# Row maxima of two score steps subtracted by four products on row tiles of 32

## The chip, the cores and the metric

The kernel runs on one core of one Trainium2 chip. The metric is the device time of one execution in microseconds. Before the change it was 839.73 us (median of 3 runs, 839.26 to 842.45).

## The reference, cut to what matters

Two batches of 1024 tokens with 128 features pass a modulated normalisation, an attention with 16 heads of 64 features, a second modulated normalisation and a mixture of 8 experts. What the change touches is the softmax of the attention:

```python
scores = jnp.einsum('bhqd,bhkd->bhqk', q, k) * scale
attn = jax.nn.softmax(scores, axis=-1)
out = jnp.einsum('bhqk,bhkd->bhqd', attn, v)
```

For each batch and head there are 1024 queries and 1024 keys. The softmax needs each query's maximum score subtracted before the exponential.

## The kernel before

**Pairs, steps and groups.** Two heads of one batch form a pair, and there are 16 pairs (`NPAIR`). The 64 features of head 0 lie on partitions 0 to 63 and those of head 1 on partitions 64 to 127. A pair's work on scores is 16 steps (`NSTEP`): 2 halves of 512 queries times 8 tiles of 128 keys. A step makes, for both heads, the scores of 128 keys (on partitions) by 512 queries in two PSUM banks. Even steps write banks 0 and 1 of `ps_s`, odd steps banks 2 and 3. Two steps form a group; a pair has 8 groups (`NGRP`), so there are 128 groups in all.

**The products of a step** (`score`, L472 to L478). q and k are each split into an upper part in TensorE's rounded float type and a rest. A step adds three products for each head, k_hi·q_hi, k_lo·q_hi and k_hi·q_lo, and a fourth, `one_row`·`neg_row` (L478), which adds minus the maximum of each query to all 128 keys. `one_row` is zero except for a row of ones at partition 0 and one at partition 64; `neg_row` holds minus the maxima of head 0 at partition 0 and of head 1 at partition 64, and zero elsewhere. Each of these products contracts over 64 partitions, so the two heads' products stand on two different halves of the array's rows and are issued one behind the other. ScalarE takes the exponential of the finished banks (`expo`, L784).

**The maxima.** A rough product of the next pair (`maxima`, L451) is reduced by VectorE (`reduce_max`, L1219), two in each group, 16 for a pair. After 8 of them, `neg_max` (L1224) gives minus the maxima of half the queries of both heads, with queries on partitions. `max_rows` on the SP queue (L1531) lays them out as rows: 8 small DMAs for a half, one for each head and 128 queries. TensorE waits for them at the first step of the half (`row_placed`).

**The order on TensorE** is written out by hand. In a group of a pair before the last it is: `maxima(p+1, 2g)`, `score(p, 2g)`, `score(p, 2g+1)`, `maxima(p+1, 2g+1)`, `up(p+2, g)` (L439, a piece of q or k of the pair after next), then the values times the probabilities of the group before (`pv`, L488). In group 0 the denominators of the pair before follow (L497), in groups 4 and 6 its outputs (L539). `maxima` waits until VectorE has reduced the one before it. The last pair has no `maxima` and no `up`, but sums of probabilities on TensorE (L506).

**The order on VectorE** in a group g of pair p: `reduce_max(p+1, 2g)`, `lower` (L1212), `reduce_max(p+1, 2g+1)`, in groups 3 and 7 `neg_max`, then `turn` (L1201 to L1206). In group 1, behind `turn`, stands `recip(p-1)` (L1261), which waits for the denominators of the pair before to have landed with queries on partitions (`den_cols_in`). In groups 3 and 5 stand `divide` (L1267).

**The order on the SP queue** for a pair p > 0: `max_rows(p, 1)`, `den_cols(p-1)` (4 DMAs, L1540, which wait for ScalarE's copy of the denominators), `inv_rows`, `inv_spread`, then `max_rows(p+1, 0)` and the weights of pair p+4. For the last pair, 8 loads of expert weights (L1558) stand between `max_rows` and `den_cols`.

**Tiles of the array.** The shapes in the profile tell which part of the array's rows a product takes: 64\*128 a product over 64 partitions, 128\*128 one over all, 128\*64 and 128\*32 products whose results go to 64 or 32 partitions, 1\*128 a product over a single partition (L690, in the experts' part).

Of the kernel before, what the change touches and what calls it, by code (L numbers as in the profile page):

```python
# [10 lines left out]
F32 = mybir.dt.float32  # L11
# [3 lines left out]
P = 128  # L15
# [3 lines left out]
TB = S // P  # L19
HP = H // 2  # L20
NPAIR = B * HP
HALF = 512
# [22 lines left out]
def ge(eng, sem, value):  # L45

    if value > 0:
        eng.wait_ge(sem, value)


def build(nc, t, out):
    ctx = ExitStack()
    with ctx:
        def sb(name, shape, dt=F32):
            return ctx.enter_context(nc.sbuf_tensor(name, shape, dt))

        def pb(name, shape=(P, HALF), dt=F32):
            return ctx.enter_context(nc.psum_tensor(name, list(shape), dt))

        def sem(name):  # L60
            return ctx.enter_context(nc.semaphore(name))
# [42 lines left out]
        q_hi = sb("q_hi", [P, 3, S], F32R)  # L104
        q_lo = sb("q_lo", [P, 3, S], F32R)
        k_hi = sb("k_hi", [P, 3, S], F32R)
        k_lo = sb("k_lo", [P, 3, S], F32R)
        hi_of, lo_of = (q_hi, k_hi), (q_lo, k_lo)
        one_row = sb("one_row", [P, P], F32R)
        neg_row = sb("neg_row", [P, 2, S], F32R)  # L110
# [66 lines left out]
        ps_s = pb("ps_s", (P, 4, HALF))  # L177
# [86 lines left out]
        s = {n: sem("s_" + n) for n in signals}  # L264
# [5 lines left out]
        row_placed = [sem(f"row_placed{n}") for n in range(2)]  # L270
# [14 lines left out]
        def n_step(p, st):  # L285
            return NSTEP * p + st + 1
# [10 lines left out]
        def n_part(p, half):  # L297
            return 2 * p + half + 1

        def n_den(p, half=0):  # L300

            return p + 1 + (half if p == LAST else 0)
# [4 lines left out]
        def quarter(j):  # L307
            return slice(32 * j, 32 * j + 32)
# [12 lines left out]
        def lowers(q):  # L321

            return (s["pool_lower"], 4) if q == 1 else (s["lower"], all_units(q))
# [25 lines left out]
        def rows(h):  # L349
            return slice(64 * h, 64 * h + 64)  # L350


        T_FEAT, T_LOG, T_CN, T_SCAT, T_DVE = (0, 2), (1, 3), 5, 3, 6

# [20 lines left out]
        def _(pe):  # L375
# [3 lines left out]
            for b in range(B):  # L379
                for n in range(2):  # L380
                    nc.tensor.matmul(ps_s[:, 2 * b + n, 0:3 * D], c_rep[:, b, :], wmod_sb[:, n * 3 * D:(n + 1) * 3 * D],
                                     start=True, stop=True).then_inc(s["mod_product"], 1)
# [59 lines left out]
            def maxima(q, n):  # L442
# [9 lines left out]
                                           k_hi[rows(h), q % 3, kh * HALF:(kh + 1) * HALF], start=True, stop=True)  # L452
                ins.then_inc(s["max_product"], 1)

            def score(p, st):

                half, kt = divmod(st, TB)
                if st == 0:
                    pe.wait_ge(*lowers(p))
                ge(pe, s["probs"], n_step(p, st) - 2)  # L460
                if kt == 0:
                    pe.wait_ge(row_placed[half], 128 * (p + 1))
                if p > 0 and st == (5 if p == LAST else 3):
                    pe.wait_ge(s["den_read"], n_den(p - 1))
                if 0 < p < LAST and st in (11, 15):
                    pe.wait_ge(s["out_added"], n_part(p - 1, st == 15))
                if p == LAST and st == 13:
                    pe.wait_ge(s["out_added"], n_part(p - 1, 0))
                kc, qc = slice(kt * P, (kt + 1) * P), slice(half * HALF, (half + 1) * HALF)
                bank = [ps_s[:, 2 * (st % 2) + h, :] for h in range(2)]  # L470
                for h in range(2):
                    nc.tensor.matmul(bank[h], k_hi[rows(h), p % 3, kc], q_hi[rows(h), p % 3, qc], start=True, stop=False)  # L472
                for h in range(2):
                    nc.tensor.matmul(bank[h], k_lo[rows(h), p % 3, kc], q_hi[rows(h), p % 3, qc], start=False, stop=False)  # L474
                for h in range(2):
                    nc.tensor.matmul(bank[h], k_hi[rows(h), p % 3, kc], q_lo[rows(h), p % 3, qc], start=False, stop=False)  # L476
                for h in range(2):
                    ins = nc.tensor.matmul(bank[h], one_row[rows(h), :], neg_row[rows(h), p % 2, qc], start=False, stop=True)  # L478
                ins.then_inc(s["scores"], 1)

            def pv(p, st):

# [121 lines left out]
            for p in range(NPAIR):  # L604
                for g in range(NGRP):
                    if p < LAST:
                        maxima(p + 1, 2 * g)
                    score(p, 2 * g)
                    score(p, 2 * g + 1)
                    if p < LAST:  # L610
                        maxima(p + 1, 2 * g + 1)
# [503 lines left out]
        def _(dve):  # L1115
            seq = [0]
            V = nc.vector

            def then(ins):

                seq[0] += 1
                ins.then_inc(s["vector_step"], 1)
                dve.wait_ge(s["vector_step"], seq[0])
# [1 line left out]
            V.memset(ones[:], 1.0)  # L1125
            V.memset(one_row[:].bitcast(F32), 0.0)
            then(V.memset(neg_row[:].bitcast(F32), 0.0))
            V.memset(one_row[0:1, :].bitcast(F32), 1.0)
            V.memset(one_row[64:65, :].bitcast(F32), 1.0).then_inc(s["constants"], 1)
            then(V.memset(head_row[:], 0.0))  # L1130
            for n in range(4):
                V.memset(head_row[32 * n:32 * n + 1, n // 2:n // 2 + 1], 1.0)
# [35 lines left out]
            for b in range(B):  # L1168
                ins = V.tensor_copy(c_rep[:, b, :], c_e[:, 0, b:b + 1].to_broadcast([P, P]))
# [50 lines left out]

            def neg_max(q, half):
                dve.wait_ge(s["max_reduced"], NMAX * q + TB * (half + 1))
                ge(dve, row_placed[half], 128 * q)
                V.tensor_reduce(nm[:, half, :, :], mx[:, :, :, 4 * half:4 * half + 4].rearrange("p h k t -> p h t k"),  # L1224
                                AX.X, ALU.max, negate=True).then_inc(s["max_row"], 1)

# [20 lines left out]
            for n in range(8):  # L1247
# [4 lines left out]
                if n == 3:  # L1252
                    inverse(T1, 4)
            neg_max(0, 0)
            for n in range(8, NMAX):
                reduce_max(0, n)
            neg_max(0, 1)

            def recip(p):
# [81 lines left out]
            row = lambda a: a.unsqueeze(1).to_broadcast([P, TB, E])  # L1341
# [77 lines left out]
            for p in range(NPAIR):  # L1419
                for g in range(NGRP):  # L1420
                    if g == 5 and 1 <= p < LAST:
                        out_add(p - 1, 0, ps_s[:, 3, :])
                    if g == 7 and 1 <= p < LAST:
                        out_add(p - 1, 1, ps_s[:, 3, :])
                    if p < LAST:
                        reduce_max(p + 1, 2 * g)
                    q, u = (p + 2, g - 1) if g else (p + 1, NGRP - 1)
                    if 2 <= q <= LAST:
                        lower(q, u)
                    if p < LAST:  # L1430
                        reduce_max(p + 1, 2 * g + 1)
                        if g % 4 == 3:
                            neg_max(p + 1, g // 4)
                    if p + 2 <= LAST:
                        turn(p + 2, g)
                    if 0 < p < LAST:
                        if g == 1:
                            recip(p - 1)
                        if g == 3:
                            divide(p - 1, 0)  # L1440
                        if g == 5:
                            divide(p - 1, 1)
                    if p == HP + 1:
                        if g in (2, 4):
                            block_stats(T0[2 * g - 4:2 * g])
                        if g == 6:
                            block_norm(T0)
            p = LAST
# [69 lines left out]
        def _(sp):  # L1518
# [4 lines left out]
            def max_rows(q, half):  # L1523

                sp.wait_ge(s["max_row"], 2 * q + half + 1)
                if q >= 2:
                    sp.wait_ge(s["scores"], n_step(q - 2, TB * half + TB - 1))
                for h in range(2):
                    for n in range(4):
                        row = neg_row[64 * h:64 * h + 1, q % 2, half * HALF + n * P:half * HALF + (n + 1) * P]  # L1530
                        sp.dma_start(row.bitcast(F32), nm[:, half, h, n:n + 1].bitcast(F32)).then_inc(row_placed[half], 16)  # L1531

            def den_cols(p, halves):
# [53 lines left out]
            weights(2)  # L1587
            sp.wait_ge(s["constants"], 1)
            max_rows(0, 0)
            max_rows(0, 1)  # L1590
            weights(3)

# [105 lines left out]
```

## Time and profile before

| | |
|---|---|
| median of 3 runs | 839.73 us |
| the profiled execution's own time | 843.6 us |
| its span from first to last instruction | 841.7 us |
| mean granted TensorE clock | 0.984 of full speed |
| PE busy | 806.4 us, 96% |
| PEld busy | 481.3 us, 57% |
| DVE busy | 618.2 us, 73% |
| ACT busy | 394.2 us, 47% |
| POOL busy | 652.0 us, 77% |
| L478 (`one_row`·`neg_row`) | 512 products, 101.4 us |
| L1531 (`max_rows`) | 256 DMAs |

PE is TensorE's matmul side and PEld its weight loads, DVE is VectorE, ACT ScalarE, POOL GpSimd, SPq the DMA queue of SyncE. The ends of matmuls are modelled, so that two of them overlap on paper; their starts are what tells their pace. L478 is line 478 of the kernel printed above.

### The profile page before, as it was taken

The page shows a single profiled execution, that of the slowest core. Times are in us where ns is not written, and L with a number is a line of the kernel's source. Part 1 is how long each engine was busy: PE and PEld are TensorE (multiplying, and loading weights), DVE is VectorE, ACT ScalarE, POOL GpSimd, SP SyncE. Part 2 cuts the span into 40 slices and gives each one's busy share as a digit, 9 for nine tenths or more (in the row PEclk, how much of TensorE's full clock was granted, in tenths as well). Part 3 has the DMA queues.
Part 4 walks back from the last instruction along what each step waited for, and adds up shares of the span by engine and source line. Part 5 has one row for each costly group of instructions (what it writes and reads, how often), then busy time and mean ns, then how long its engine had stood idle before and what let it go on. Part 6 is the DMA issues. An engine that isn't in the chain of part 4 may idle for free.

```text
span 841.7 us, 15143 instructions
## 1 busy us (share of the span) xinstructions
PE 806.4 (96%) x5218; PEld 481.3 (57%) x5218; DVE 618.2 (73%) x1204; ACT 394.2 (47%) x636; POOL 652.0 (77%) x341
## 2 busy tenths in 40 slices
PE   4878999999999999999999999999999999999986
PEld 2535556555555555555555555555565555448886
DVE  8887777787778787878777877778777756346644
ACT  3655444444444444444444445544444444435543
POOL 3479998999999797979797989888888787041654
PEclk8979999999999999999999999999999999999989
DMA  9600010101001010101010101010101010452763
GB/s 246 144 1 14 14 27 14 28 14 25 15 13 28 2 39 2 38 3 39 1 39 2 39 1 40 1 27 15 28 1 27 1 27 1 127 181 80 243 217 97
DMA packets 83257, 40.00 MB, mean 48 GB/s; under 512 B 57433, under 2 KB 71136, under 8 KB 83120
## 3 DMA queue, kind: packets, MB, share of 16 engines
q1 hardware_dynamic: 81456, 35.86, 17.9%
q0 software_dynamic: 1728, 3.19, 1.0%
q8 instruction: 43, 0.70, 0.3%
q14 instruction: 30, 0.25, 0.1%
HBM read 31.46 MB, written 8.21 MB: 47 GB/s over the span
## 4 chain that ended last, share of the span: by engine, by line
PE 93%; DVE 3%; DMA 1%; issue 1%; POOL 1%; ACT 0%; POOLq 0%; SPq 0%; DVEq 0%
PE ps_o L488 28%; PE ps_m L451 9%; PE ps_x L439 9%; PE ps_s L472 7%; PE ps_s L474 7%; PE ps_s L478 7%; PE ps_s L476 7%; PE ps_s L539 4%; PE ps_s L677 3%; PE ps_s L497 2%; DVE mx L1219 1%; PE ps_m L506 1%; PE ps_s L687 1%; PE ps_x L687 1%; PE ps_o L687 1%
## 5 line engine op out<-in xcount | busy, mean ns | idle before, releaser
L1040 POOL TENSOR_TENSOR big<-big,probs 128x1024 f32<-128x1024 f32 x180 | 440.3, 2446 | 70.0 <-ACT probs L784 49.9
L1219 DVE TENSOR_REDUCE mx<-ps_m 128x2 f32<-128x1024 f32 x240 | 294.0, 1225 | 108.5 <-PE ps_m L451 108.2
L784 ACT ACTIVATE probs<-ps_s 128x1024 f32<-128x1024 f32 x256 | 248.9, 1024 | 169.1 <-PE ps_s L478 169.0
L488 PE MATMUL ps_o<-probs,c_all 128*64 128x512 f32 x1024 | 247.9, 605 | 0.0
L488 PEld LDWEIGHTS ps_o<-probs,c_all 128*64 128x64 f32 x1024 | 62.1, 136 | 97.2 <-ACT probs L784 41.4
L451 PE MATMUL ps_m<-k_hi,q_hi 64*128 64x512 f32 x480 | 108.4, 444 | 2.2 <-DVE mx L1219 2.2
L472 PE MATMUL ps_s<-q_hi,k_hi 64*128 64x512 f32 x512 | 101.8, 393 | 0.0
L478 PE MATMUL ps_s<-neg_row,one_row 64*128 64x512 f32 x512 | 101.4, 388 | 0.0
L474 PE MATMUL ps_s<-q_hi,k_lo 64*128 64x512 f32 x512 | 101.2, 390 | 0.0
L476 PE MATMUL ps_s<-q_lo,k_hi 64*128 64x512 f32 x512 | 101.2, 389 | 0.0
L451 PEld LDWEIGHTS ps_m<-k_hi,q_hi 64*128 64x128 f32 x480 | 46.6, 183 | 87.3 <-issue 77.0
L1040 POOL TENSOR_TENSOR big<-probs 128x1024 f32<-128x1024 f32 x30 | 71.6, 2386 | 9.9 <-ACT probs L784 9.9
L775 ACT CAST q_hi<-ps_x 128x256 fp32r<-128x256 f32 x56 | 20.9, 372 | 90.6 <-DVE ps_x L1206 90.6
L478 PEld LDWEIGHTS ps_s<-neg_row,one_row 64*128 64x128 f32 x512 | 48.8, 184 | 10.5
L476 PEld LDWEIGHTS ps_s<-q_lo,k_hi 64*128 64x128 f32 x512 | 48.4, 184 | 10.7
L474 PEld LDWEIGHTS ps_s<-q_hi,k_lo 64*128 64x128 f32 x512 | 48.4, 184 | 10.3
L472 PEld LDWEIGHTS ps_s<-q_hi,k_hi 64*128 64x128 f32 x512 | 48.6, 185 | 9.6 <-issue 3.3
L1102 POOL DMA_INDIRECT out_dram<-c_all,token x30 | 29.8, 993 | 29.1 <-DVE c_all L1483 20.9
L1206 DVE TENSOR_TENSOR ps_x<-ps_x,big 128x256 f32<-128x256 f32 x112 | 48.5, 433 | 3.8
L1276 DVE TENSOR_TENSOR h<-h,ps_s 128x512 f32<-128x512 f32 x29 | 20.0, 688 | 40.2 <-PE ps_s L539 39.6
L1201 DVE TENSOR_TENSOR ps_x<-ps_x,big 128x256 f32<-128x256 f32 x112 | 47.3, 423 | 0.0
L1204 DVE TENSOR_TENSOR big<-ps_x,big 128x256 f32<-128x256 f32 (+1 forms) x113 | 47.2, 417 | 0.0
(310 smaller groups left out, 997.3 us busy)
## 6 DMA issues: line engine op xcount, KB each, us to landing
big<-in_experts SPq DMA_DIRECT2D x30, 322.0 KB, 3.6
big<-rd_dram SPq DMA_DIRECT2D x60, 128.0 KB, 2.9
big<-in_wqk SPq DMA_DIRECT2D x16, 256.0 KB, 2.7
neg_row<-nm SPq DMA_DIRECT2D x256, 0.5 KB, 2.0
xs_row<-xs_dram SPq DMA_DIRECT2D x6, 390.0 KB, 4.2
big<-in_expert_w SPq DMA_DIRECT2D x8, 256.0 KB, 4.0
xs_dram<-zero SPq DMA_DIRECT2D x2, 990.0 KB, 10.4
xs_dram<-zero SPq DMA_DIRECT2D x2, 960.0 KB, 11.7
```

The lines of the kernel that those rows point to most:

```text
L439: ins = nc.tensor.matmul(bank, m[:, q % 2, w, twin, :], src, start=(n == 0), stop=(n == 1))
L451: ins = nc.tensor.matmul(bank[:, h, :], q_hi[rows(h), q % 3, qt * P:(qt + 1) * P], k_hi[rows(h), q % 3, kh * HALF:(kh + 1) * HALF], start= ...
L472: nc.tensor.matmul(bank[h], k_hi[rows(h), p % 3, kc], q_hi[rows(h), p % 3, qc], start=True, stop=False)
L474: nc.tensor.matmul(bank[h], k_lo[rows(h), p % 3, kc], q_hi[rows(h), p % 3, qc], start=False, stop=False)
L476: nc.tensor.matmul(bank[h], k_hi[rows(h), p % 3, kc], q_lo[rows(h), p % 3, qc], start=False, stop=False)
L478: ins = nc.tensor.matmul(bank[h], one_row[rows(h), :], neg_row[rows(h), p % 2, qc], start=False, stop=True)
L488: ins = nc.tensor.matmul(ps_o[64 * h:64 * h + 64, :], c_all[:, (p // HP) * TB + kt, :], probs[:, st % 4, h, :], start=(kt == 0), stop=(kt ...
L784: nc.scalar.activation(probs[:, st % 4, :, :], ps_s[:, 2 * (st % 2):2 * (st % 2) + 2, :], ACT.Exp, scale=SCALE).then_inc(s["probs"], 1)
L1040: V.tensor_tensor(acc[:, buf(p, half), :, :], first, probs[:, st % 4, :, :], ALU.add).then_inc(s["added"], 1)
L1201: V.tensor_tensor(straight, straight, cos_sb[:, c], ALU.mult).then_inc(s["turned"], 1)
L1206: V.tensor_tensor(straight, straight, part, ALU.add).then_inc(s["rotated"], 1)
L1219: V.reduce_max(mx[:, :, kh, qt], max_banks(q, n), AX.X).then_inc(s["max_reduced"], 1)
```

## The change

The constants: `one_row` has a row of ones at each of the partitions 0, 32, 64 and 96. `max_rows` places the negated maxima of head 0 at partitions 0 and 32, and those of head 1 at 64 and 96, for every pair but the first; for the first only at 0 and 64 as before. A half of a pair thus has 16 small DMAs in place of 8, and the counts that wait on them follow (`n_rows`).

On TensorE the two products at L478 go from each step. In their place `less_max` stands at the start of the odd step, behind that step's waits. It issues four products, each over 32 partitions: two that end the even step's banks, and two that begin the odd step's banks. In pairs after the first these four stand on the four different row tiles of 32; in the first pair the even and the odd step's stand on the same two. The wait for `row_placed` moves into `less_max`. The even step's signal is given by the second of the four, and the odd step's by its last k_hi·q_lo.

```diff
+        def n_rows(q):
+            return 128 * (2 * q + 1)
...
+            def less_max(p, st, steps):
+                half = st // TB
+                qc = slice(half * HALF, (half + 1) * HALF)
+                if st % TB == 0:
+                    pe.wait_ge(row_placed[half], n_rows(p))
+                for odd in steps:
+                    for h in range(2):
+                        r = quarter(2 * h + odd if p else 2 * h)
+                        ins = nc.tensor.matmul(ps_s[:, 2 * odd + h, :], one_row[r, :], neg_row[r, p % 2, qc],
+                                               start=(odd == 1), stop=(odd == 0))
+                    if odd == 0:
+                        ins.then_inc(s["scores"], 1)
...
-                if kt == 0:
-                    pe.wait_ge(row_placed[half], 128 * (p + 1))
...
+                odd = st % 2
+                if odd:
+                    less_max(p, st - 1, (0, 1))
                 for h in range(2):
-                    nc.tensor.matmul(bank[h], k_hi[rows(h), p % 3, kc], q_hi[rows(h), p % 3, qc], start=True, stop=False)
+                    nc.tensor.matmul(bank[h], k_hi[rows(h), p % 3, kc], q_hi[rows(h), p % 3, qc], start=not odd, stop=False)
...
-                    nc.tensor.matmul(bank[h], k_hi[rows(h), p % 3, kc], q_lo[rows(h), p % 3, qc], start=False, stop=False)
-                for h in range(2):
-                    ins = nc.tensor.matmul(bank[h], one_row[rows(h), :], neg_row[rows(h), p % 2, qc], start=False, stop=True)
-                ins.then_inc(s["scores"], 1)
+                    ins = nc.tensor.matmul(bank[h], k_hi[rows(h), p % 3, kc], q_lo[rows(h), p % 3, qc], start=False, stop=bool(odd))
+                if odd:
+                    ins.then_inc(s["scores"], 1)
...
-            V.memset(one_row[0:1, :].bitcast(F32), 1.0)
-            V.memset(one_row[64:65, :].bitcast(F32), 1.0).then_inc(s["constants"], 1)
+            for j in range(4):
+                ins = V.memset(one_row[32 * j:32 * j + 1, :].bitcast(F32), 1.0)
+            ins.then_inc(s["constants"], 1)
...
-                ge(dve, row_placed[half], 128 * q)
+                ge(dve, row_placed[half], n_rows(q - 1) if q else 0)
...
-                for h in range(2):
+                for j in (range(4) if q else (0, 2)):
+                    h = j // 2
                     for n in range(4):
-                        row = neg_row[64 * h:64 * h + 1, q % 2, half * HALF + n * P:half * HALF + (n + 1) * P]
+                        row = neg_row[32 * j:32 * j + 1, q % 2, half * HALF + n * P:half * HALF + (n + 1) * P]
```

## Rows read from the trace of the kernel before

**Rows 1.** The page: TensorE's granted clock in 40 slices, in tenths.
```profile
PEclk8979999999999999999999999999999999999989
```

**Rows 2.** The page: the chain that ended last, by engine and by line.
```profile
PE 93%; DVE 3%; DMA 1%; issue 1%; POOL 1%; ACT 0%; POOLq 0%; SPq 0%; DVEq 0%
PE ps_o L488 28%; PE ps_m L451 9%; PE ps_x L439 9%; PE ps_s L472 7%; PE ps_s L474 7%; PE ps_s L478 7%; PE ps_s L476 7%; PE ps_s L539 4%; PE ps_s L677 3%; PE ps_s L497 2%; DVE mx L1219 1%; PE ps_m L506 1%; PE ps_s L687 1%; PE ps_x L687 1%; PE ps_o L687 1%
```

**Rows 3.** Timeline of PE, groups 1 and 2 of a pair: start us, us, instruction, count.
```profile
330.78 0.40 PE L478 MATMUL ps_s<-neg_row,one_row 64*128 64x512 f32 x2
331.01 0.40 PE L451 MATMUL ps_m<-k_hi,q_hi 64*128 64x512 f32 x2
331.34 0.39 PE L439 MATMUL ps_x<-ck,wh 128*128 128x256 f32 x1
331.56 0.28 PE L439 MATMUL ps_x<-ck,wl 128*128 128x256 f32 x1
331.68 0.29 PE L439 MATMUL ps_x<-ck,wh 128*128 128x256 f32 x1
...
332.01 1.94 PE L488 MATMUL ps_o<-probs,c_all 128*64 128x512 f32 x8
333.88 0.50 PE L451 MATMUL ps_m<-k_hi,q_hi 64*128 64x512 f32 x2
334.21 0.39 PE L472 MATMUL ps_s<-q_hi,k_hi 64*128 64x512 f32 x2
...
336.04 0.43 PE L451 MATMUL ps_m<-k_hi,q_hi 64*128 64x512 f32 x2
```

**Rows 4.** Timeline of PE, four products on column tiles of 32.
```profile
110.17 1.06 PE L497 MATMUL ps_s<-big,ones 128*32 128x512 f32 x8
```

**Rows 5.** Timeline of PE, a product over one partition, then products over 128.
```profile
765.17 0.48 PE L690 MATMUL ps_s<-big,ones_sq 1*128 1x128 f32 x2
765.59 1.06 PE L592 MATMUL ps_m<-gw_sb,h2T 128*128 128x8 f32 x8
766.50 1.14 PE L677 MATMUL ps_s<-moe,big 128*128 128x128 f32 x8
```

**Rows 6.** Timeline of the SP queue in the pair of rows 3, and in the last pair.
```profile
321.83 4.99 SPq L1531 DMA_DIRECT2D neg_row<-nm  x8
329.58 2.46 SPq L1540 DMA_DIRECT2D denc<-den  x4
...
712.44 5.16 SPq L1531 DMA_DIRECT2D neg_row<-nm  x8
717.71 4.79 SPq L1558 DMA_DIRECT2D big<-in_expert_w  x8
```

**Rows 7.** Timeline of DVE in the pair of rows 3.
```profile
333.72 0.24 DVE L1261 RECIPROCAL rc<-denc 128x16 f32<-128x16 f32 x1
334.42 1.23 DVE L1219 TENSOR_REDUCE mx<-ps_m 128x2 f32<-128x1024 f32 x1 [0.46 <-PE ps_m L451]
```

**Rows 8.** Timelines of SP, DVE and PE in the last pair but one.
```profile
670.23 4.98 SPq L1531 DMA_DIRECT2D neg_row<-nm  x8
677.30 2.46 SPq L1540 DMA_DIRECT2D denc<-den  x4
681.25 0.25 DVE L1261 RECIPROCAL rc<-denc 128x16 f32<-128x16 f32 x1 [0.85 <-DMA denc<-den]
683.71 0.39 PE L451 MATMUL ps_m<-k_hi,q_hi 64*128 64x512 f32 x2
```

**Rows 9.** Timelines of DVE and PE where PE waits for a reduction.
```profile
68.39 1.23 DVE L1219 TENSOR_REDUCE mx<-ps_m 128x2 f32<-128x1024 f32 x1 [0.83 <-PE ps_m L451]
69.77 0.50 PE L451 MATMUL ps_m<-k_hi,q_hi 64*128 64x512 f32 x2 [0.75 <-DVE mx L1219]
```

**Rows 10.** Timelines of DVE and PE in the last pair.
```profile
737.58 1.29 DVE L1267 TENSOR_TENSOR ou<-ou,big 128x512 f32<-128x512 f32 x2
742.74 1.16 PE L539 MATMUL ps_s<-hT,ou 128*128 128x128 f32 x8
```

## Prediction, made before the changed kernel had run

> **What bounds the kernel now.** I read the chain of waits on the page first. 93% of the span runs through PE, and the lines on it are the ones that the change edits and their neighbours: L472 to L478 have 7% each [rows 2]. The clock row says that this PE runs at the higher of its two levels (2.4 GHz) in nearly all slices [rows 1]. Then I read the timeline of PE through one group, by starts, since ends are modelled. No gap in it is left that another engine causes; the pace is that of PE's own products. So whatever the change takes from or adds to PE's row of starts in a group counts in full, 128 times. Last I read the SP queue and VectorE between two pairs, because the change doubles DMAs there [rows 6 to 8].
>
> **The slot.** Two products of 64 partitions and 512 columns, one for each head, start together, and the next two start 0.23 us later (330.78 to 331.01) [rows 3]. A step has four such slots, so a group has eight, and the two of L478 are worth 0.46 us. The four products of 32 partitions go to four different row tiles and four banks. The nearest row is the one where four products go to four column tiles: its 8 records (4 products in 2 passes) take 1.06 us, where 8 records of L488 on two tiles (four passes) take 1.94 [rows 3, 4]. Four tiles run beside each other as well as two. I take one slot of 0.23 us for the four. The bounds: 0.23, and 0.46 if only two at a time run. Removed, then: 0.46 - 0.23 = 0.23 us in each group after the first pair (15 x 8 = 120 groups), nothing in the first pair's 8 groups, where the four stand on two tiles and need two slots.
>
> **The change of tile size, twice in a group.** No row of before shows a step from 64 rows to 32 and back, but all changes of the tile's shape that the rows show cost alike. From L451 (64\*128) to L439 (128\*128): 331.01 to 331.34 is 0.33, which is 0.10 over the slot, and the first L439 takes 0.22 to the second, which takes 0.12 to the third: 0.10 more. Together 0.20 us. Behind L488 (128\*64) the first L451 (64\*128) takes 0.33 in place of 0.23 (333.88 to 334.21), the same second part [rows 3]. A product over one partition between products over 128 is the row nearest to tiles of 32. From its start, with its weights in the open and the emptying behind it, to the next line it takes 0.42 us (765.17 to 765.59), for two passes, where the passes behind it take 0.91 / 8 = 0.11 each: 0.20 over once more [rows 5]. I read it as two parts: the array empties (0.09 to 0.10), and the first weights of the new shape are loaded in the open, not under the product before (0.10 to 0.11). Two changes in a group cost 2 x 0.20 = 0.40 us. Bounds for one change: 0 (tiles of 64 and of 32 rows might count as one kind), and 0.25 (as above with four loads in the open in place of one or two). I take 0.20, where all the shape changes in the rows lie.
>
> In sum, a group of the later 15 pairs gets 0.40 - 0.23 = 0.17 us longer, one of the first pair 0.40. That is 120 x 0.17 = 20.4 (21 with 0.175) and 8 x 0.40 = 3.2, **24 us in all**.
>
> The Trainium skill (TensorEngine Tiling (Array Packing), Key Properties) says the same in a rule: a switch of tiling mode, not of the tile alone, drains the TensorE, and its list has rows of 64 and of 32 as two modes. The trace agrees for the changes it has, with 0.20 us each [rows 3, 5]. Against it stands another page of the Trainium skill (TensorE: Matmul & The Clock Gate, What overlaps and what doesn't), which has four tiles of 32 rows start about 4 ns apart and weights load under products on other row groups; by it alone a group would be 0.23 us shorter. No run here has shown that for a change of shape.
>
> **The even step's signal** comes from the second of the four, at about the place of its old fourth slot, 0.2 us later by the first change of shape. The odd step's comes 0.17 later. ScalarE and GpSimd follow; the products that need these probabilities (L488) stand one group later, some 5 us. Cost 0. The waits of the odd step (bank read, `den_read`, `out_added`) now stand before the even step is ended, but what they wait for is released by earlier work. Cost 0, at most some 0.1 us in three groups of a pair. The wait for `row_placed` comes 0.7 us later in the group than before: gain 0, as nobody waited there. The two more memsets are about 0.1 us on VectorE at the start, under the loads of the inputs.
>
> **The doubled DMAs.** On the SP queue 8 of them take 4.99 us and 4 of the next kind 2.46, so one more is 0.63 to 0.64 [rows 6]. Bounds: 0.63, and 0 if the issue were not what holds the queue; its constant pace says it is. 16 then take 4.99 + 8 x 0.64 = 10.1 us. Behind them in the queue stand the four `denc<-den` (L1540), which had started at 329.58, when ScalarE's copy was there. Now the queue is free at 321.83 + 10.1 + 0.1 (the step from 717.60 to 717.71 [rows 6]) = 332.07. From the first of these four to the reciprocal it takes 3.95 us where VectorE did nothing but wait (677.30 to 681.25 [rows 8]). So the reciprocal of this pair starts at 336.02 in place of 333.72 [rows 7], 2.3 us later, and VectorE waits at it. What is queued behind it on VectorE is `reduce_max`, due at 334.42. It starts at 336.2, takes 1.23 and ends at 337.43; from such an end to the L451 that waits for it it takes 0.15 (68.39 + 1.23 = 69.62, then 69.77) [rows 9], so PE goes on at 337.58. PE had reached this L451 at 336.04 [rows 3], and with three groups' products 0.175 longer reaches it at 336.57. **PE waits 1.0 us**, in pairs 1 to 13. In pair 14 the same sum gives: queue free at 670.23 + 10.24 = 680.47, reciprocal at 684.42, PE free at 685.98, due at 683.71 + 0.53 = 684.24, so 1.7 us [rows 8]. Together 13 x 1.0 + 1.7 = **15 us**. Bounds: 0 (if the later queue is hidden) to 18, if the queue's way to the first of L1540 is 0.2 us longer in each pair.
>
> Later in the pair nothing is late: all is moved by the same wait, and the queue's next task, `max_rows(p+1, 0)`, has until the pair's end. `row_placed` of half 1 lands 12 us after the first issue and is wanted in group 4, some 20 us after it. In the last pair the expert weights and L1540 start 5.1 us later. VectorE has no maxima left; its divisions at 737.58 come at latest at 742.7 and end at 744.0, and L539 wants them at 742.74 + 5 x 0.175 = 743.6 [rows 10]: at most 0.4 us, which I put at 0.
>
> **The sum.** 24 + 15 = 39 us. Against the profiled execution's own time, 843.6 (span 841.7 and 1.9 around it), that is 882.6. That execution was 3.9 us above the median of the three runs, and the sum goes on the median: 839.7 + 39 = **879 us**.
>
> **Rivals.**
> - Switching costs, but the longer queue is hidden, because VectorE or the landing has slack that I don't see: 839.7 + 24 = 864 us. For it: of these pairs only the one of rows 8 lists a wait at L1261. Against it: the reciprocal starts only 4.14 us behind the first L1540 there, of which 3.95 is the bare way, so the slack was 0.19 us [rows 6 to 8].
> - Tiles of 64 and of 32 rows are one kind, and the change of shape is free, but the queue is late. The products save 120 x 0.23 = 27.6 us. PE is then due at the L451 at 336.04 - 0.69 = 335.35 and waits 2.2 us in 13 pairs and 3.0 in pair 14, 32 us together. Result 844, not clearly slower. For it: no row shows 64 to 32. Against it: the three kinds of change that rows show.
> - The shape change is free and the queue is hidden: 839.7 - 27.6 = 812 us, clearly faster. This needs both; it decides in every group, from a switch of under 0.11 us on, as 2 x 0.115 is the slot that is saved. The same price of 0.20 in all rows speaks against it.
>
> **Chances.** The forecast 0.60; queue hidden (864) 0.14; shape free, queue late (844) 0.13; both free (812) 0.08; something that makes it longer than 890, such as four tiles in two slots (120 x 0.23 = 28 more), 0.05. The forecast's own range is 866 to 890: switches of 0.15 (12 us less) to 0.25, where the queue's wait shrinks as the groups get longer. The range that holds 8 in 10 reaches down to the rival at 844, so 841 to 890. A measurement of this kernel can tell 0.5% (4 us) from no change. Faster by more than that: 0.09. Within: 0.07, which is half of the rival at 844. Slower: 0.84.
>
> **What would show it.** In PE's timeline of a group: the four products start within some 20 ns, 0.33 us behind the last L476, and the next two starts are 0.33 us apart each; a group without extras (334.21 back to the one before at 329 or so) lasts 5.2 us, not 5.03. 16 issues of `neg_row<-nm` take 10.1 us, and the waits list VectorE's reciprocal waiting for `denc<-den` in all pairs, then L451 waiting about 1 us for L1219 in group 2. If the four start 0.23 us behind L476 and the k_hi·q_hi 0.23 us behind them, the switch is free and the forecast wrong; if the L451 of group 2 has no wait, its second part is.

## The result, and the profile after

The changed kernel takes 894.1 us (median of 4 runs, 889.24 to 898.75), the kernel before beside it 840.51. The ratio is 1.0622, with a 95% interval of 1.0583 to 1.066: **slower by 6%**, 53.6 us, where the forecast was 879 and 39 us. The direction and both mechanisms came out as forecast. The sum was too small, and the time lies above the range, which ended at 890.

The chain of waits on the page of the changed kernel, and TensorE's granted clock in 40 slices, which answer to [rows 1, 2]:

```profile
PEclk8979999999999999999999999999999999999999
...
PE 64%; SPq 19%; DVE 8%; DMA 5%; issue 3%; POOL 0%; ACT 0%; POOLq 0%; DVEq 0%
```

PE had 93% of the chain before; now 19% of it is the SP queue, which had nothing. The chain goes back from PE over VectorE to the queue wherever PE waited last. The slices are too coarse to show what the clock did; a window further down does.

PE's timeline of groups 1 and 2 of a pair, as in [rows 3] (start us, us, instruction, count):

```profile
350.28 0.40 PE L491 MATMUL ps_s<-q_hi,k_hi 64*128 64x512 f32 x2
...
355.16 0.50 PE L455 MATMUL ps_m<-k_hi,q_hi 64*128 64x512 f32 x2
355.50 0.40 PE L491 MATMUL ps_s<-q_hi,k_hi 64*128 64x512 f32 x2
...
355.98 0.40 PE L495 MATMUL ps_s<-q_lo,k_hi 64*128 64x512 f32 x2
356.30 0.51 PE L468 MATMUL ps_s<-neg_row,one_row 32*128 32x512 f32 x4
356.74 0.50 PE L491 MATMUL ps_s<-q_hi,k_hi 64*128 64x512 f32 x2
357.08 0.40 PE L493 MATMUL ps_s<-q_hi,k_lo 64*128 64x512 f32 x2
357.31 0.40 PE L495 MATMUL ps_s<-q_lo,k_hi 64*128 64x512 f32 x2
358.40 0.50 PE L455 MATMUL ps_m<-k_hi,q_hi 64*128 64x512 f32 x2 [0.70 <-DVE mx L1238]
```

The four products of L468 are one row and one slot. Into them it takes 0.32 us (355.98 to 356.30), out of them 0.44 (356.30 to 356.74), and the next slot takes 0.34, where each was 0.23. That is 0.09 + 0.21 + 0.11 = 0.41 us for two changes of the tile's shape. The weight loads (PEld) show the part in the open: those of L468 start at the same time as its first product, 356.30, and not under the product before.

```profile
356.30 0.19 PEld L468 LDWEIGHTS ps_s<-neg_row,one_row 32*128 32x128 f32 x4 [0.37 <-issue]
```

The group lasts 5.22 us (350.28 to 355.50), where it was 5.05. Then the second half of the forecast: L455 would have followed L495 after 0.23 us, at 357.54, and starts at 358.40.

The same place on the SP queue and on VectorE, as in [rows 6, 7]:

```profile
342.74 10.13 SPq L1551 DMA_DIRECT2D neg_row<-nm  x16
352.97 2.48 SPq L1560 DMA_DIRECT2D denc<-den  x4
```
```profile
356.93 0.25 DVE L1280 RECIPROCAL rc<-denc 128x16 f32<-128x16 f32 x1 [1.83 <-DMA denc<-den]
357.10 1.16 DVE L1238 TENSOR_REDUCE mx<-ps_m 128x2 f32<-128x1024 f32 x1
```

The 16 DMAs take 10.13 us (forecast 10.1), the reciprocal starts 14.19 us after the first of them (forecast 14.19), and L455 15.66 (forecast 15.75). The list of waits of the whole kernel (us in total, times, longest) has them as its own rows:

```profile
DVE rc L1280 <- DMA denc<-den: 45.3, 15, 11.6
...
PE ps_m L455 <- DVE mx L1238: 18.6, 16, 1.8
```

What the forecast did not have is in another pair, here pair 5. SP queue, VectorE, PE:

```profile
294.26 11.00 SPq L1551 DMA_DIRECT2D neg_row<-nm  x16
```
```profile
309.34 0.25 DVE L1280 RECIPROCAL rc<-denc 128x16 f32<-128x16 f32 x1 [2.71 <-DMA denc<-den]
```
```profile
310.82 0.68 PE L455 MATMUL ps_m<-k_hi,q_hi 64*128 64x512 f32 x2 [1.58 <-DVE mx L1238]
311.43 0.58 PE L443 MATMUL ps_x<-cq,wh 128*128 128x256 f32 x1
311.81 0.41 PE L443 MATMUL ps_x<-cq,wl 128*128 128x256 f32 x1
312.02 0.41 PE L443 MATMUL ps_x<-cq,wh 128*128 128x256 f32 x1
```

One of these 16 issues took 1.47 us in place of 0.60, so the whole row takes 11.00. L455 starts 16.56 us after the first issue. Behind it the slots of L443 are 0.21 us apart, where they were 0.12. Two stretches of 3.2 and 3.4 us tell why. A line has the busy times of PE, PEld, DVE, ACT and POOL, then the granted clock, the DMA share and GB/s:

```profile
311.10:314.30 3.20, 3.20 (x10) 1.46 (x10) 2.34 (x4) 0.36 (x1) 3.06 (x2) 0.50 0.01 3
317.00:320.40 3.40, 3.40 (x20) 1.58 (x20) 2.63 (x7) 1.94 (x2) 2.30 (x1) 1.00 0.01 2
```

In the first, right behind L455, the granted clock is 0.50, the lower of its two levels (1.2 GHz). In the second, 2.7 us after the first has ended, it is 1.00 (2.4 GHz) again. PE had stood still for 1.6 us just before the first.

**Where the time went.** I took the start of each group in both traces and compared their distances. From the first group to the last the changed kernel is 52.0 us longer:

| part | forecast, us | measured, us |
|---|---|---|
| products and changes of shape: 0.14 to 0.23 in nearly every group of pairs 1 to 15, 0.4 in pair 0 | 24 | 25.6 |
| wait of L455 in group 2 of pairs 1 to 14 | 15 | 19.3 |
| its weights in the open behind the wait: the next product follows it after 0.43 in place of 0.33 | 0 | 1.2 |
| half clock behind the wait, in pairs 1, 5 and 14, 1.5 to 1.7 each | 0 | 4.8 |
| half clock in the first group of pair 0 | 0 | 1.1 |

The wait is L455's start minus the start that it has where nobody waits (14.80 us after the first issue, from e1 below; 14.02 in pair 14), which gives 13 x 1.33 + 1.97. The last row is not laid to the change, since e4 below, which has neither small tiles nor more DMAs, has 1.6 us there. The start is 2.1 us and the end 1.1 us shorter, which leaves the 48.8 us between the two spans. The profiled run before was 3.1 us above its median and this one 1.7 below, which makes the 53.6 of the medians.

### The profile page after: what moved, and what is told of

It reads as the page before. It is cut to its first block, busy times and chain, and to the rows that moved or that the text cites. A ratio compares the mean times of both kernels' runs of the same rounds, so it can differ in the third digit from the quotient of the medians.

```text
span 890.5 us, 15399 instructions
## 1 busy us (share of the span) xinstructions
PE 840.8 (94%) x5218; PEld 447.3 (50%) x5218; DVE 616.7 (69%) x1206; ACT 395.2 (44%) x636; POOL 650.7 (73%) x341
## 4 chain that ended last, share of the span: by engine, by line
PE 64%; SPq 19%; DVE 8%; DMA 5%; issue 3%; POOL 0%; ACT 0%; POOLq 0%; DVEq 0%
PE ps_o L506 18%; SPq L1551 15%; PE ps_m L455 7%; PE ps_s L491 7%; PE ps_x L443 5%; DVE mx L1238 5%; PE ps_s L495 5%; PE ps_s L493 5%; PE ps_s L468 4%; PE ps_s L557 4%; DMA denc<-den 3%; SPq L1560 3%; PE ps_s L695 2%; PE ps_m L524 1%; DMA hT<-xs_dram 1%
## 5 line engine op out<-in xcount | busy, mean ns | idle before, releaser
L506 PE MATMUL ps_o<-probs,c_all 128*64 128x512 f32 x1024 | 251.7, 613 | 0.0
L455 PE MATMUL ps_m<-k_hi,q_hi 64*128 64x512 f32 x480 | 109.6, 452 | 18.6 <-DVE mx L1238 18.6
L491 PE MATMUL ps_s<-q_hi,k_hi 64*128 64x512 f32 x512 | 116.3, 450 | 0.0
L495 PE MATMUL ps_s<-q_lo,k_hi 64*128 64x512 f32 x512 | 101.8, 393 | 0.0
L455 PEld LDWEIGHTS ps_m<-k_hi,q_hi 64*128 64x128 f32 x480 | 45.5, 184 | 107.7 <-issue 99.5
L468 PE MATMUL ps_s<-neg_row,one_row 32*128 32x512 f32 x512 | 66.8, 493 | 0.0
L491 PEld LDWEIGHTS ps_s<-q_hi,k_hi 64*128 64x128 f32 x512 | 48.2, 185 | 36.6 <-issue 35.8
L495 PEld LDWEIGHTS ps_s<-q_lo,k_hi 64*128 64x128 f32 x512 | 48.7, 185 | 11.4
L493 PEld LDWEIGHTS ps_s<-q_hi,k_lo 64*128 64x128 f32 x512 | 48.8, 186 | 5.4
L468 PEld LDWEIGHTS ps_s<-neg_row,one_row 32*128 32x128 f32 x512 | 25.3, 181 | 46.9 <-issue 46.9
```

The lines of the kernel that those rows point to most:

```text
L455: ins = nc.tensor.matmul(bank[:, h, :], q_hi[rows(h), q % 3, qt * P:(qt + 1) * P], k_hi[rows(h), q % 3, kh * HALF:(kh + 1) * HALF], start= ...
L468: ins = nc.tensor.matmul(ps_s[:, 2 * odd + h, :], one_row[r, :], neg_row[r, p % 2, qc], start=(odd == 1), stop=(odd == 0))
L495: ins = nc.tensor.matmul(bank[h], k_hi[rows(h), p % 3, kc], q_lo[rows(h), p % 3, qc], start=False, stop=bool(odd))
L506: ins = nc.tensor.matmul(ps_o[64 * h:64 * h + 64, :], c_all[:, (p // HP) * TB + kt, :], probs[:, st % 4, h, :], start=(kt == 0), stop=(kt ...
```

## The experiments

They ran on other chips, on which the kernel before took 854 to 856 us. The ratios are what compares. The difference between the chips lies outside the attention for the most part: in e4's trace, 14.3 us longer than that of the kernel before, 10.2 us lie behind the start of the last group and 1.1 ahead of the first. 1.6 are the half clock in pair 0. The other groups agree within 0.05 us but for one with 0.15, so distances between groups can be set beside those of the kernel before.

**e1, the queue put right.** 12 of the 16 DMAs stay ahead of the denominators, 4 go into a gap of the queue.

```diff
-                    max_rows(p, 1)
+                    max_rows(p, 1, (0, 2, 1, 3) if p == LAST else (0, 2, 1))
...
                     inv_rows(p - 1, (0, 1))
+                    if p < LAST:
+                        max_rows(p, 1, (3,))
                     inv_spread(p - 1, (0, 1))
```

> The changed kernel, but max_rows(p, 1) of pairs 1 to 14 is issued as 12 DMAs ahead of the denominators' columns and 4 between rd_dram and its spread, so that the denominators' columns leave the queue at their old time. Theory A (products some 26 us, late queue some 20 us, a lower TensorE clock after the waits some 5 to 8 us): no wait in group 2, reciprocal at its old place, no added stretch at half clock, 840.5 + 26 = 866 us, 863 to 869. Rival B (the excess over the forecast lies in the products, e.g. pieces of groups that the longer order makes late elsewhere): 875 or more. Rival C (the dips of the clock come from the changes of tile shape): dips in the attention stay, 870 to 880.

Measured: 886.5 us against 854.1, ratio 1.0396 (1.0336 to 1.0455). SP, VectorE and PE in pair 6:

```profile
331.57 7.56 SPq L1551 DMA_DIRECT2D neg_row<-nm  x12
339.52 2.46 SPq L1560 DMA_DIRECT2D denc<-den  x4
...
344.59 2.44 SPq L1551 DMA_DIRECT2D neg_row<-nm  x4
```
```profile
343.84 0.24 DVE L1280 RECIPROCAL rc<-denc 128x16 f32<-128x16 f32 x1
```
```profile
346.14 0.40 PE L495 MATMUL ps_s<-q_lo,k_hi 64*128 64x512 f32 x2
346.38 0.39 PE L455 MATMUL ps_m<-k_hi,q_hi 64*128 64x512 f32 x2
```

L455 follows L495 in its slot. Group 2 is 0.17 to 0.19 us longer than before in all 14 pairs, like its neighbours, and no stretch at low clock lies between 70 and 770 us. From the first group to the last e1 is 31.3 us longer than the kernel before. 25.3 of it are the products, which settles that term, and 1.0 is half clock in pair 0. The remaining 4.9 us fall at one place in the last pair, where L468 now stands behind a wait for the output's addition, with half clock behind it:

```profile
770.23 0.40 PE L495 MATMUL ps_s<-q_lo,k_hi 64*128 64x512 f32 x2
772.85 0.80 PE L468 MATMUL ps_s<-neg_row,one_row 32*128 32x512 f32 x4 [2.22 <-DVE h L1295]
```

VectorE did that addition 4.0 us after its products had ended, and the records don't say what for. e5, which has the same DMAs, has it too (4.2 us), e2 a shorter one (2.5), the others none, so the cause stays open. It is most of the distance from the expected 866 / 840.5 = 1.030.

**e2, the doubled DMAs alone**, in the kernel before: `n_rows` and the loop over four rows from the change, nothing on TensorE.

```diff
-                for h in range(2):
+                for j in (range(4) if q else (0, 2)):
+                    h = j // 2
                     for n in range(4):
-                        row = neg_row[64 * h:64 * h + 1, q % 2, half * HALF + n * P:half * HALF + (n + 1) * P]
+                        row = neg_row[32 * j:32 * j + 1, q % 2, half * HALF + n * P:half * HALF + (n + 1) * P]
```

> The kernel before with nothing but the doubled DMAs (rows at 32 and 96 too, where one_row is zero). Theory A: the reciprocal of pairs 1 to 14 comes some 14.2 us after the first issue, L451 of group 2 at 15.7 or more in place of 14.2, so a wait of 1.5 to 2.4 us in 13 pairs and 2.2 or more in pair 14, 22 to 34 us in all, and stretches at half clock may follow: 862 to 880 us. Rival (the queue costs nothing by itself and it is the longer groups that bring the waits): 840 to 843 us.

Measured: 901.7 us, ratio 1.0579 (1.0521 to 1.0637), 48 us over the kernel before.

```profile
339.35 10.15 SPq L1535 DMA_DIRECT2D neg_row<-nm  x16
349.60 2.48 SPq L1544 DMA_DIRECT2D denc<-den  x4
```
```profile
353.31 0.42 PE L481 MATMUL ps_s<-neg_row,one_row 64*128 64x512 f32 x2
355.04 0.50 PE L454 MATMUL ps_m<-k_hi,q_hi 64*128 64x512 f32 x2 [1.31 <-DVE mx L1222]
```

240 DMAs of half a KB each, whose data add nothing to the result, cost nearly as much as the whole change. Group 2 is longer by 1.55 to 1.58 us where all issues were regular: L454 starts 15.69 us after the first issue and was due at 14.20, and 0.07 are its weights in the open. It is longer by 2.0 where something in the queue was late, by 3.8 to 4.2 in six pairs where the clock fell too, and by 3.4 in pair 14, with 0.5 more in the group behind. An eighth stretch at half clock stands in group 4 of pair 8, behind a wait of 1.9 us for a division that took 2.93 us; e3 and e7 tell of such divisions. Per pair e2 waits longer than the change, whose longer groups bring L455 0.6 us later (due at 14.80 in place of 14.20).

**e3, the change of shape alone.** Two row tiles of 32 in all pairs, two slots, no doubled DMAs.

```diff
-                        r = quarter(2 * h + odd if p else 2 * h)
+                        r = quarter(2 * h)
...
-                for j in (range(4) if q else (0, 2)):
+                for j in (0, 2):
```

> The changed kernel with the placement of its first pair in all pairs: the four products stand on two row tiles of 32, two slots of 0.23 us, and the DMAs are not doubled. It has two changes of shape in each of 128 groups and saves no slot. Theory A: 128 x 0.40 to 0.43 = 51 to 55 us more, 892 to 896 us, with no wait at the reciprocal and no dips of the clock in the attention. Rival (a change from 64 to 32 rows is cheaper than the others, and the queue made the loss): under 870 us.

Measured: 934.1 us, ratio 1.0929 (1.0887 to 1.0972), 80 us. 0.39 to 0.44 us in nearly every group agrees with two changes of 0.20, some 52 us. The rest was not expected: group 4 of pairs 1 to 13 is 1.96 us longer, and 3.6 in three of them, where the clock fell as well. VectorE, GpSimd and PE in pair 6:

```profile
375.69 2.72 DVE L1286 TENSOR_TENSOR ou<-ou,big 128x512 f32<-128x512 f32 x1
378.34 1.22 DVE L1238 TENSOR_REDUCE mx<-ps_m 128x2 f32<-128x1024 f32 x1
```
```profile
372.98 4.89 POOL L1058 TENSOR_TENSOR big<-big,probs 128x1024 f32<-128x1024 f32 x2 [0.55 <-ACT probs L802]
```
```profile
376.80 0.73 PE L468 MATMUL ps_s<-neg_row,one_row 32*128 32x512 f32 x4
377.46 0.49 PE L491 MATMUL ps_s<-q_hi,k_hi 64*128 64x512 f32 x2
...
379.70 0.50 PE L455 MATMUL ps_m<-k_hi,q_hi 64*128 64x512 f32 x2 [1.28 <-DVE mx L1238]
```

The division, 0.68 us elsewhere, takes 2.72 and ends some 0.5 us after GpSimd's second add, which had started just ahead of it (the first of the two ends at 375.4). e7 tests that.

**e4, the new order with tiles of 64.** `r = rows(h)`, no doubled DMAs, no change of shape.

> The changed order with tiles of 64: four products over 64 partitions between the two steps' other products, two slots, no change of shape, DMAs not doubled. Theory A: 8 slots as before, 840.5 us within 0.3%, so that place and start/stop flags cost nothing. Rival (the later end of the even step, or the odd step's waits ahead of it, cost by themselves): 845 or more.

Measured: 855.9 us against 854.5, ratio 1.0009 (0.9993 to 1.0025). Place, flags and the moved waits cost nothing that can be told.

**e5, one change of shape in place of two.** The DMAs as in e1, the four products just ahead of `up`.

```diff
-                odd = st % 2
-                if odd:
-                    less_max(p, st - 1, (0, 1))
...
                         maxima(p + 1, 2 * g + 1)
+                    less_max(p, 2 * g, (0, 1))
```

> Split DMAs as in e1, and the four products over 32 partitions moved behind the second maxima of the group, just ahead of the products over 128 partitions (in the last pair ahead of those on 32 columns), where the shape changes anyway: one more change of shape in a group, not two. Theory A: 120 x (0.20 - 0.23) = -3 us and 8 x 0.20 = +2 us, 839 to 842 us, no change that can be told. Rival (32 to 128 costs more than 64 to 128, or the exponentials come too late): 850 or more.

Measured: 922.6 us, ratio 1.0801 (1.0764 to 1.0837). A miss, the worst but one. VectorE, then PE, in group 3 of a pair:

```profile
364.56 1.23 DVE L1233 TENSOR_REDUCE mx<-ps_m 128x2 f32<-128x1024 f32 x1 [1.06 <-PE ps_m L455]
```
```profile
365.51 0.39 PE L491 MATMUL ps_s<-q_lo,k_hi 64*128 64x512 f32 x2
365.94 0.50 PE L455 MATMUL ps_m<-k_hi,q_hi 64*128 64x512 f32 x2
366.37 0.50 PE L468 MATMUL ps_s<-neg_row,one_row 32*128 32x512 f32 x4
366.80 0.38 PE L443 MATMUL ps_x<-ck,wh 128*128 128x256 f32 x1
```

With six slots between the two `maxima` of a group in place of eight, the second is due at 365.74 and the reduction ends only at 365.79, plus 0.15 to PE. So 0.2 us are lost in a group, and 0.1 more since L455's weights are loaded in the open behind the wait: groups 0 to 3 are 0.25 to 0.30 us longer than before. The order before had 0.39 us between that end and L451, which I had not looked at when I moved the slot. Groups 5 and 7 are 0.44 longer, groups 4 and 6 some 1.25: all 26 divisions of pairs 1 to 13 take 2.0 to 2.2 us here. They meet GpSimd's adds, as in e3: in this pair the division runs from 368.94 to 370.94, and an add that had started at 368.02 ends at some 370.5. The price of the change of shape itself is again as before: 0.43 into `up`, 0.20 over a slot.

**e6, the reciprocal put behind the reduction** of group 2 on VectorE; all else as in the change.

```diff
                         reduce_max(p + 1, 2 * g)
+                        if p > 0 and g == 2:
+                            recip(p - 1)
...
-                        if g == 1:
-                            recip(p - 1)
```

> The changed kernel, with the reciprocal of pairs 1 to 14 put behind the reduction of group 2 on VectorE, not ahead of it. The queue is as late as in the changed kernel. Theory A (what costs is that reduce_max stands behind the reciprocal): the wait of L455 in group 2 is gone, VectorE waits less, 866 us, 863 to 870. Rival (the late denominators cost elsewhere, at the divisions or the outputs): 872 or more, with waits at L557 or in groups 3 to 5.

Measured: 905.5 us, ratio 1.0613 (1.0567 to 1.0659), no gain that the intervals can tell (1.0622 and, in e8, 1.0656 for the change). Group by group the mechanism holds: the extra in group 2 falls from 25.3 us to 4.4 in all. It comes back elsewhere, 10.8 us in group 4 of pairs 2, 7 and 8 and 1.6 in pair 14. VectorE, GpSimd and PE in pair 8:

```profile
461.99 2.81 DVE L1286 TENSOR_TENSOR ou<-ou,big 128x512 f32<-128x512 f32 x1
```
```profile
459.34 4.91 POOL L1058 TENSOR_TENSOR big<-big,probs 128x1024 f32<-128x1024 f32 x2 [0.75 <-ACT probs L802]
```
```profile
466.07 0.72 PE L455 MATMUL ps_m<-k_hi,q_hi 64*128 64x512 f32 x2 [1.74 <-DVE mx L1238]
466.73 0.58 PE L443 MATMUL ps_x<-ck,wh 128*128 128x256 f32 x1
```

The later reciprocal has shifted VectorE against GpSimd, the division misses the seam between two adds, and PE waits and then runs at the low clock (L443 after 0.66 us). Another 5.3 us are low clock in pair 0, over 13.7 us. e7 has as much, where the other runs have 2.3 or less, and neither's edit touches that pair.

**e7, e3 with the first division 1.3 us earlier** on VectorE, ahead of `turn`.

> The kernel of e3 (two changes of shape in each group, no doubled DMAs), with the first division of a pair moved ahead of turn in group 3 on VectorE, about 1.3 us earlier. In e3 that division took 2.72 us in 13 pairs in place of 0.68 and ended just behind an add on GpSimd that was running all the while, and PE then waited 1.3 us in group 4. Theory A (the division is held by the add on GpSimd, so that its place against the adds sets its price): it now comes near the seam between two adds and is held for a shorter time, PE's wait of group 4 goes in most pairs: 13 x 1.55 = 20 us less than e3, and some 2 to 6 more where the clock no longer falls, 1.062 to 1.072 of the kernel before. Rival (the division waits for its data or is slow for another reason): still 2 us or more, 1.09.

Measured: 914.0 us, ratio 1.0661 (1.0608 to 1.0714), against 1.0929 of e3.

```profile
370.38 1.32 DVE L1286 TENSOR_TENSOR ou<-ou,big 128x512 f32<-128x512 f32 x1
```
```profile
368.79 5.16 POOL L1058 TENSOR_TENSOR big<-big,probs 128x1024 f32<-128x1024 f32 x2 [0.56 <-ACT probs L802]
```
```profile
373.83 0.40 PE L495 MATMUL ps_s<-q_lo,k_hi 64*128 64x512 f32 x2
374.10 0.50 PE L455 MATMUL ps_m<-k_hi,q_hi 64*128 64x512 f32 x2
```

The division takes 1.32 us in all 13 pairs, GpSimd's two adds 0.27 more than in e3, and PE does not wait. Group 4 is 0.56 us longer than before the change, not 1.96. One instruction in another place gives back 0.027 of 856, some 23 us, so the division's place against the adds set its price.

**e8, the changed kernel on such a chip.**

> The changed kernel itself once more, unchanged, on the same chip as e7, so that its ratio can be set beside those of the experiments, which ran on chips where the kernel before takes 854 us. Theory A: the loss is the same in us: 1.06 of the kernel before, with 8 or so of the queues' 16 issues late by 0.3 to 1 us and a few stretches at half clock in group 2 of other pairs than before. Rival (the loss depends on the chip): under 1.05 or over 1.07.

Measured: 911.1 us against 856.4, ratio 1.0656 (1.0619 to 1.0693), the same loss. The late issues fall in the same pairs as in the first profile (2, 4, 5, 8, 11, 12, 14), the low clock in pairs 1, 2, 4, 5 and 11: five pairs, where the first profile had three, two of them the same.

## Why the prediction was wrong

**What bounds the kernel** was right. Whatever changed in PE's row of starts counted in full, in every run.

**The slot** was right: four products on four row tiles take one slot, 0.23 us (0.44 from L468 to the next, less the 0.21 of a change of shape). e3 (two slots) and e1 (one) differ by 0.22 us in a group.

**The change of tile size, twice in a group**: forecast 24 us, measured 25.6, and 25.3 in e1. The price of 0.20 us, taken from shapes other than these, held for 64 to 32 rows and back. The rival in which that change is free is refuted, since L468 starts 0.32 and L491 0.44 us behind its forerunner. With that goes what the Trainium skill's rule on weights loaded under products of other row groups (TensorE: Matmul & The Clock Gate, What overlaps and what doesn't) would have made of this change: here L468's weights were not loaded before its first product, at 356.30. The Trainium skill's rule that a switch of tiling mode drains the TensorE (TensorEngine Tiling (Array Packing), Key Properties) agrees with the trace, by the 0.09 us ahead of L468.

**The even step's signal and the moved waits**, forecast 0: right, by e4. The two more memsets take 0.17 us each, 0.23 apart, not 0.1 together; they stand at 3.8 us of the span and the start is not longer.

**The doubled DMAs**: the first of two steps that failed, by its size: forecast 15 us, measured 19.3 and the 1.2 of the weights. The mechanism was right down to the 0.1 us where the queue was regular: L455 at 15.67 to 15.69 us in four pairs, forecast 15.75. But I wrote that the pace of the issues was constant, and gave an upper bound of 18 us for 0.2 us more in a pair. In seven of 14 pairs one of the 16 issues took 0.92 to 1.51 us in place of 0.60, and in three more the queue or the landing was late without such a row. The trace of before had the warning, in the pair ahead of that of [rows 6]:

```profile
278.30 5.89 SPq L1531 DMA_DIRECT2D neg_row<-nm  x8
286.04 2.46 SPq L1540 DMA_DIRECT2D denc<-den  x4
```

One of these eight issues takes 1.51 us. It cost nothing there, because the queue otherwise stands idle for 2.8 us before `denc<-den` and still had 1.8 left. The change used that up, and then the queue's irregularity stood on the path.

**The sum** is the second: it left out a term, what PE's waits do to its clock, and so put it at nothing without a reason. It is 4.8 us in the profile, in three of the 14 pairs, and more in other runs: the four runs of the change have mean granted clocks of 0.985, 0.979, 0.975 and 0.973 and spans of 887.3, 890.5, 893.8 and 896.8 us. The kernel before kept the higher level through the whole attention (57 to 801 us in its profile). A reading of what a wait costs has to include the stretch behind it.

**The rivals.** "Queue hidden" (864) is refuted by e2, which has nothing but the queue. What I had against it, a slack of 0.19 us, was right. The two with a free change of shape (844 and 812) fall with L468's 0.32 us. The time did come out longer than 890, but not by what I had named for that, four tiles in two slots.

No version came out that beats the kernel before. e1 is the best with tiles of 32, and it is 4.0% slower. The reason is arithmetic: a slot is worth 0.23 us and a change of shape 0.20, so two changes for one slot lose 0.17 us in a group, and one change, as in e5, could gain at most 0.03.

## What to carry to other kernels

Count the changes of tile shape in the order of TensorE as instructions with a price (0.20 us here, nearly the 0.23 of a product with 512 columns); packing products more tightly pays only if it saves more slots than it adds changes. Before adding small DMAs to a queue, find what stands behind them and which engine stands still for it: slack of a few us in the queue is what hides its irregular issues. And price a wait of TensorE of a us or more with the slow stretch that can follow it.

## What the runs showed of the hardware that was not expected

- **A division on VectorE that waits for GpSimd.** `ou` times `big`, both in SBUF, takes 0.68 us alone, and 2.0 to 2.93 us in e2, e3, e5 and e6, where, in the traces shown, an add on GpSimd had started ahead of it. Where it comes at the seam between two adds it slips in, as in e7, and GpSimd's adds take longer instead. The Trainium skill (SBUF — State Buffer, SBUF: two separate sides) says that the two engines share a pair of ports as an exclusive lock, and that a VectorE instruction with two SBUF inputs takes part in it against GpSimd's reads. The traces agree: the division ends 0.54 us behind the add in e3 and 0.55 in e6.
- **The clock falls after short waits of TensorE**, of 1.2 to 2.3 us, but not after each: in group 2 behind 3 of 14 in the first profile of the change, 5 in the second, 7 in e2. Each such stretch lasts 3.4 us and costs 1.5 to 1.7. In e3, e6 and e7 one in pair 14 stands behind no wait but behind 16 products of 8 columns (L610). What tells which wait is followed by one stays open.
- **An issue on the SP queue can take 0.9 to 1.7 us in place of 0.60**, some 15 times in 496, in the same pairs in both runs of the change. What delays it was not tried.
